# Making the last chunk's residual behind the first split instead of behind the second, in the transition from attention to experts

## The reference

```python
x = x + _L0_attn_ref(_layernorm(x), W_write, W_read, decay, log_alpha)
x = x + _L0_ffn_ref(_layernorm(x), gate_w, w1, b1, w2, b2)
```

## Time and profile before

| | us |
|---|---|
| median of 3 runs | 562.24 |
| the three runs | 560.73, 562.24, 564.35 |
| the profiled execution, its whole time | 562.67 |
| its span, first to last instruction | 560.9 |

### The profile page before, as it was taken

How to read it: one execution, slowest core, us unless ns; L and a number is a source line. 1 busy time by engine, 2 the same in 40 slices (tenths; PEclk the granted TensorE clock), 3 DMA queues, 4 the chain that set the end, 5 groups by cost and what they waited for, 6 DMA issues and landing times.

```text
span 560.9 us, 17645 instructions
## 1 busy us (share of the span) xinstructions
PE 530.1 (95%) x5234; PEld 415.3 (74%) x5234; DVE 448.4 (80%) x1375; ACT 338.3 (60%) x856; POOL 246.9 (44%) x291
## 2 busy tenths in 40 slices
PE   7799899999999999999999999999999999999991
PEld 7677778778786777777777777777777777777770
DVE  4889999999987689868768787688777777778861
ACT  6899989898745876445545554455544544545540
POOL 5625778888746084523223233223322333322433
PEclk9999999999998999999999999999999999999997
DMA  5576867777345396433263364343344454344323
GB/s 161 201 229 225 258 185 234 210 222 231 126 105 129 87 216 101 71 60 62 51 103 56 53 105 77 63 68 61 61 63 79 78 78 75 68 64 67 63 37 36
DMA packets 85096, 63.33 MB, mean 113 GB/s; under 512 B 54224, under 2 KB 77392, under 8 KB 85008
## 3 DMA queue, kind: packets, MB, share of 16 engines
q1 hardware_dynamic: 71328, 43.94, 32.3%
q0 software_dynamic: 13392, 18.27, 17.3%
q10 hardware_dynamic: 288, 0.00, 0.0%
HBM read 37.56 MB, written 24.62 MB: 111 GB/s over the span
## 4 chain that ended last, share of the span: by engine, by line
PE 77%; DVE 10%; issue 4%; DMA 3%; ACT 2%; POOL 1%; SPq 1%; POOLq 0%; DVEq 0%; ACTq 0%
PE psum L1697 32%; PE psum L1712 21%; PE psum L1714 10%; PE psum L1509 3%; DVE weights L874 2%; PE psum L1592 2%; PE psum L1573 2%; PE psum L1599 2%; PE psum L1520 2%; DVE arena L1052 1%; PE psum L1559 1%; DMA arena<-sent_rows 1%; PE psum L1612 1%; PE psum L1496 1%; DVE arena L1063 1%
## 5 line engine op out<-in xcount | busy, mean ns | idle before, releaser
L1697 PE MATMUL psum<-arena,weights 128*128 128x256 f16 (+1 forms) x2208 | 279.7, 249 | 1.1 <-DVE arena L1316 1.0
L1697 PEld LDWEIGHTS psum<-arena,weights 128*128 x2208 | 187.4, 98 | 79.3 <-issue 4.1
L589 POOL DMA_INDIRECT out<-arena,tile_in x71 | 115.0, 1619 | 233.4 <-DVE arena L1343 126.9
L1712 PE MATMUL psum<-weights,arena 128*128 x556 | 211.7, 381 | 0.0
L826 ACT ACTIVATE arena<-psum,b_cur 128x256 f32<-128x256 f32 (+1 forms) x368 | 131.4, 423 | 129.9 <-PE psum L1697 115.6
L1714 PE MATMUL psum<-weights,arena 128*128 x556 | 152.0, 273 | 0.0
L1327 DVE TENSOR_TENSOR arena<-arena 128x512 f16<-128x512 f32 x142 | 98.5, 694 | 10.8 <-ACT arena L843 6.3
L559 POOL DMA_INDIRECT sent_rows<-arena,tiny x64 | 65.4, 1022 | 35.5 <-issue 17.8
L1323 DVE CAST arena<-arena 128x512 f16<-128x512 f32 x126 | 53.5, 424 | 8.8 <-ACT arena L826 8.5
L1712 PEld LDWEIGHTS psum<-weights,arena 128*128 128x128 f16 x556 | 54.4, 98 | 5.0
L1714 PEld LDWEIGHTS psum<-weights,arena 128*128 128x128 f16 x556 | 54.5, 98 | 4.6
(11 more groups left out here) (199 smaller groups left out, 642.9 us busy)
## 6 DMA issues: line engine op xcount, KB each, us to landing
weights<-in_experts SPq DMA_DIRECT2D x32, 512.0 KB, 4.8
arena<-sent_rows SPq DMA_DIRECT2D x100, 64.0 KB
arena<-in_b SPq DMA_DIRECT2D x46, 128.0 KB, 3.2
arena<-in_x SPq DMA_DIRECT2D x16, 256.0 KB, 3.4
out<-arena SPq DMA_DIRECT2D x16, 256.0 KB, 4.1
arena<-sent_rows SPq DMA_DIRECT2D x84, 32.0 KB
sent_rows<-pad SPq DMA_DIRECT2D x7, 265.0 KB, 4.6
tile_in<-sent_rows SPq DMA_DIRECT2D x71, 4.5 KB, 2.6
```

Of the source, the lines that this page charges most:

```text
L589: pool.indirect_dma_start(out=out, out_offset=bass.IndirectOffsetOnAxis(ap=at_u, axis=0), in_=yout[:, u % 4], in_offset=None, compute_op=A ...
L1697: last = pe.matmul(ps_h[:, f % 2, mm * n:(mm + 1) * n], w1_of(e_of[i], k, lo, per * (f - GROUP[i]) + mm), turned[:, i % 2, part, k, 0:n], ...
L1712: pe.matmul(to, h_hi[:, z % 4, at], w2_of(e_of[t], m), start=(m == 0), stop=(m == MF - 1), skip_group_check=True)
```

## The change

In VectorE's order the residual of chunk 15 stands directly behind `split(0)`, and ahead of `split(1)` and `low_tile(1)`. Its statistics and moments stay where they are. No instruction is added or removed, no wait and no buffer is changed, and the other engines' orders stay as they are.

```diff
             last_step()
             m = NCH - 3
             split(0)
+            residual(NCH - 1)
             split(1)
             low_tile(1)
-            residual(NCH - 1)
             residual_stats(NCH - 1)
             residual_moments(NCH - 1)
             place(m)
```

## The result

| | before | after |
|---|---|---|
| median, 22 runs each | 562.78 us | 559.85 us |
| lowest to highest | 560.12 to 566.03 | 558.77 to 563.07 |
| ratio after to before | | 0.9957, 95% interval 0.994 to 0.9974 |
| profiled execution: time, span | 562.67, 560.9 | 558.79, 557.0 |

The ratio is a gain of 2.4 us (0.0043 x 562.78), with an interval from 1.5 to 3.4 us; the two medians are 2.9 us apart. The gain is clear of noise, and it is less than one per cent.

What follows compares the result with a forecast made beforehand. Stage two was taken as bound by TensorE, so an earlier start brings the end forward. Terms 1.25 + 1.67 - 0.15 = 2.77 us, from the median 562.24 us of three runs, gave 559.5 us, range 557.8 to 562.2.

Steps and rivals of the forecast that it cites:

- The residual: On VectorE, L985 of chunk 15 starts behind split(0) at about 172.45 without waiting, margin 0.3 us, and ends at 173.13.
- TensorE's wait: The idle time in front of rank(13), spent waiting for the residual, goes: 1.25 us gained, bounds 0 and 1.36.
- The clock: Without the idle time, TensorE's clock does not fall to half in pair(3, 0): 1.67 us gained, bounds 0 and 1.67.
- The new wait at `rank(14)`: TensorE, arriving earlier, waits for VectorE's mask of chunk 14 in front of rank(14): 0.15 us lost.
- The rest: split(1) and low_tile(1) come 0.31 us later, with 2.8 us slack before pair(4, 1); the gain there reaches the end.
- the fall stays: Rival: the gap before rank(13) goes, but pair(3, 0) still takes 4.28 us at half clock; gain 1.25, 561.0 us; chance 0.15.
- The wait is not L985's: Rival: rank(13) waits for something other than the residual, or another wait takes over; gain 0 to 0.3 us, 562.1; chance 0.06.
- Slower, the slow stretch moves: Rival: small work and rank(14)'s wait bring half clock over pair(3, 0) and pair(4, 1); 0.4 us slower, 562.7; chance 0.05.

Runs made afterwards that it cites:

- e8: The changed kernel, unchanged, run again on chip B: 576.81 us, ratio 0.9991 to the kernel before.
- e9: The changed kernel, unchanged, run again on chip C: 560.56 us, ratio 0.9968 to the kernel before.
- e12: Kernel before, with rank(13) in a PSUM bank of its own and no wait for the residual, on chip C: 561.17 us, ratio 0.9982.
- e4: Changed kernel, with rank(13) also waiting for the statistics of chunk 15, on chip A: 575.52 us, ratio 1.0045 to the kernel before.
- e7: The kernel before, unchanged, run again on chip B: 578.87 us, ratio 1.0004 to the kernel before.
- e11: Changed kernel, with rank(13) also waiting for the statistics of chunk 15, on chip C: 562.66 us, ratio 1.0007 to the kernel before.
- e2: Kernel before, with the residual moved up one place only, between split(1) and low_tile(1), on chip A: 575.85 us, ratio 1.0004.
- e3: Kernel before, with rank(13) in a PSUM bank of its own and no wait for the residual, on chip A: 574.14 us, ratio 1.0031.
- e5: Kernel before, with rank(13) and score_experts(14) swapped on TensorE, on chip B: 577.28 us, ratio 1.0016.
- e10: Changed kernel, with 16 tiny activations added at ScalarE's start, on chip C: 561.00 us, ratio 0.9984 to the kernel before.
- e1: Kernel before, with 18 small matmuls on TensorE between pair(2) and rank(13), the wait kept, on chip A: 575.40 us, ratio 1.0033.
- e6: Changed kernel, with low_tile(1) moved behind the choice of chunk 14, on chip B: 576.46 us, ratio 0.9992 to the kernel before.

## Why the prediction was right, point by point

It forecast 559.5 us, in a range of 557.8 to 562.2, as 2.77 us below the kernel before. Measured were 559.85 us, and 2.4 us by the ratio. The medians are 2.9 us apart. The trace gives 2.80 us at the place where the sum was made, term by term:

- *The residual.* Forecast: starts right behind `split(0)`, without a wait. It does (171.11 + 0.77 = 171.88), here and on chip C. On chips A and B it waits about 1 us (see e8): the margin of 0.3 us did not hold there.
- *TensorE's wait.* Forecast 1.25 us. From `pair(2)` to `pair(3, 0)` it was 176.25 - 172.58 = 3.67 us and is 174.42 - 172.12 = 2.30: 1.37 us, at the upper bound of 1.36. The bracket's 1.20 us was short because it counts from the modelled end of the last matmul; starts are the better measure.
- *The clock.* Forecast 1.67 us. `pair(3, 0)` now has 174.42 to 177.03 (one step of 0.11 behind L1714), 2.61 us, against 4.28: 1.67 us, to the hundredth.
- *The new wait at `rank(14)`.* Forecast 0.15 us. From 177.03 to `pair(4, 1)` at 177.37 it takes 0.34 us, before it took 0.10: 0.24 us. This term was too small by 0.09 us. The wait itself was as forecast: 0.13 us, from 177.03 to the rank at 177.16, and VectorE's mask too (it ends at 177.10, 4.98 us behind the start of `pair(2)`; forecast 177.70 - 172.58 = 5.12). What was left out stands behind the rank: from it to `pair(4, 1)` it takes 0.21 us where it took 0.10. After the waits of e8, e9 and e12 it is 0.21 to 0.22 as well; why is not shown.
- *The rest.* `split(1)` and the low tile came later and nobody waited for them, and from 185 us on TensorE is full.

1.37 + 1.67 - 0.24 = 2.80 us. That the sum is off by only 0.03 us is partly luck: one term was too small by 0.12, the other by 0.09 with the opposite sign. The mechanism was right in each. What the prediction called the least that a measurement can tell, one per cent, was too careful: the interval of the ratio is 0.17% to either side, and 0.4% was clear of noise.

The weakest term is the clock, which the sum took in full. It is 1.67 us only in an execution in which the kernel before has the fall. Over all profiles of this case, the half clock was there in `pair(3, 0)` in each of the four with 1.17 us of idle or more (before, e4, e7, e11), and in none of the ten with 0.92 or less. But the clock doesn't hang on the idle time alone. In e7 TensorE idles for 1.17 us twice: in front of `pair(0)`, with a dense product behind it, the clock stays at 1.00; in front of `rank(13)`, with 1.0 us of small matmuls behind it, the clock falls. And the same place can go either way. At `score_experts(15)` on chip A e2 idled 1.35 us and kept 1.00, while e3 idled 1.18 us and fell to 0.50; on chip B e5 and e8 idled 1.53 and fell.

How often the kernel before has the fall is not shown; its two profiles both have it. The mean clock of a whole execution can't settle it. One fall is 0.003 of it (0.990 in the profiled execution of before, 0.993 in that of after), but there are falls elsewhere. Here are the changed kernel's two profiles, after and then e9, between 12 and 20 us, columns as in the earlier trace rows:

```profile
12.00:20.00 8.00, 5.26 (x88) 4.25 (x87) 4.37 (x10) 5.54 (x17) 6.55 (x17) 1.00 0.40 115
...
12.00:20.00 8.00, 5.26 (x59) 3.86 (x58) 4.16 (x10) 4.13 (x14) 6.55 (x17) 0.79 0.32 105
```

The kernel is the same and TensorE is busy for the same 5.26 us, but the clock is full in one and falls in the other. On chip C the 35 executions of before lie between 0.984 and 0.993 with a mean of 0.9881, the 12 of e9 between 0.986 and 0.994 with a mean of 0.990, and the 12 of e10, in the same order, have 0.9884. Three executions of before have 0.993, as high as the profile of after, in which the clock is full until close to the end; there the fall is probably missing. In such an execution the gain would be 1.37 - 0.24 = 1.13 us, an estimate from the terms above. The measured 2.4 and 1.8 us lie between that and 2.80.

The Trainium skill ("TensorE: Matmul & The Clock Gate", Part 1, What's actually happening) has the half rate come after an idle window. The prediction gave the case that follows from a strict reading, that the fall stays, 0.15. The traces don't bear that reading out: with 1.20, 1.17 and 1.70 us of idle followed by small work the clock fell, and when only that idle was filled (e1) it did not. The same section's other statement, that the control runs free of the kernel's start, would allow what e2 and e3 show; no run here tests it.

The rivals: "the fall stays" is refuted by the profile of after, by e9 and by e12, and e1 and e11 show from both sides that the idle time matters. "The wait is not L985's" is refuted by e12, where taking that one wait out ends the idle time. "Slower, the slow stretch moves" did not happen in the main comparison nor on chip C, but it is the rival that came nearest to something real: on chip B (e8) the half clock did turn up three pairs later, in `pair(6, 3)`, behind another idle time. It was priced at the wrong place, `rank(14)`; the wait that can take the gain is the one of `score_experts(15)` for ScalarE.

## What to carry to other kernels

Idle time that names "issue" can have a releaser all the same, as here: list what the instruction waits for in the code, and look which of these ended 0.1 us before, on its own engine and at other engines that wait for the same event. When a short idle of TensorE stands beside small matmuls, look at the granted clock behind it before pricing it; here the slow pair behind a wait of 1.20 us cost 1.67 us on top of it. And look for the next instruction on the path that hangs on another engine's queue: in the profiles on chip B a gain of 1.63 us at `pair(4, 1)` was gone at `pair(6, 3)`, because ScalarE was late in between.

## What the runs showed of the hardware that I had not expected

The same kernel took 562.8 us in the main comparison and 561.95 on chip C, but 572.8 on chip A and 577.4 on chip B. The profiles on chips A and B show holds of ScalarE for which the profile names no releaser in the core (it writes "remote"), one of them in seven of the eight in front of L712 or its like (3.0 to 4.4 us; in the eighth, e6, the 5.2 us there are put down to "issue"). The row of e7:

```profile
169.19 0.60 ACT L712 ACTIVATE arena<-psum 128x512 f32<-128x512 f32 x1 [4.39 <-remote]
```

Neither the two profiles of the main comparison nor the four on chip C have such a row on ScalarE. What makes these holds is open. Whether the edit, worth 0.4% in the main comparison, is worth less on chips A and B is open too: its own step works in the profile of e8, and the interval there is too wide to tell.
